# Phase stage of a four-layer kernel: sums and residual moved to GpSimd, gates and branch weights in column strips, all engine orders rewritten

## What is computed

```python
pos_cos, pos_sin = cos(pos_phases[:L]), sin(pos_phases[:L])
pos_values = x @ Wpv + bpv
pos_mem_cos = cumsum(pos_cos * pos_values, axis=1)
pos_mem_sin = cumsum(pos_sin * pos_values, axis=1)
pos_ret = (pos_cos * pos_mem_cos + pos_sin * pos_mem_sin) / sqrtD
key_ph = tanh(x @ Wk + bk) * pi
key_cos, key_sin = cos(key_ph), sin(key_ph)
kv_values = x @ Wkv + bkv
gh = gelu(concatenate([x, _shift1(x)], -1) @ Wg1 + bg1)
value_gates = sigmoid(gh @ Wg2 + bg2)                      # one number per token
kv_mem_cos = cumsum(_shift1(key_cos) * kv_values * value_gates, axis=1)
kv_mem_sin = cumsum(_shift1(key_sin) * kv_values * value_gates, axis=1)
gate_cumsum = maximum(cumsum(value_gates, axis=1), 1.0)
kv_ret = (key_cos * kv_mem_cos + key_sin * kv_mem_sin) / (sqrt(gate_cumsum) * sqrtD)
bw = softmax(gelu(x @ Wb1 + bb1) @ Wb2 + bb2)              # two numbers per token
blended = bw[..., 0:1] * pos_ret + bw[..., 1:2] * kv_ret
ln = (blended - mean) / sqrt(var + 1e-5) * ln_g + ln_b
return x + ln @ Wo + bo
```

## Time and profile before

| | |
|---|---|
| median of 3 runs | 4881.25 us (4877.01 to 4888.4) |
| profiled execution | 4887.22 us, span 4885.4 us, mean granted TensorE clock 0.962 |
| busy in the span | TensorE 4556.5, VectorE 3270.8, ScalarE 2206.4, GpSimd 1148.4 us |
| phase stage | from 2663.2 (its first DMA) to 3252.07 us (first DMA of the next stage) |

### The profile page before, as it was taken

One profiled execution on the slowest core, in us unless ns is written; L12 is line 12 of the kernel. 1 busy time (PEld: TensorE's weight loads), 2 busy tenths in 40 slices (PEclk: granted clock), 3 DMA queues, 4 the chain that ended last, 5 costly groups with the idle time before them and its releaser, 6 DMA issues. The chain is left out here.

```text
span 4885.4 us, 96760 instructions
## 1 busy us (share of the span) xinstructions
PE 4556.5 (93%) x40984; PEld 3133.7 (64%) x40984; DVE 3270.8 (67%) x3874; ACT 2206.4 (45%) x3585; POOL 1148.4 (24%) x854
## 2 busy tenths in 40 slices
PE   8699999999999996999996999949999999999999
PEld 5334444444333334888884455539999999988888
DVE  7599888887889861462223899956766666644443
ACT  3157777777677672323222555522222222233333
POOL 3512322222312202444441000003333333300000
PEclk9889999999999998999998999979999999999999
DMA  5544453544444316343344122256444444455553
GB/s 179 152 65 60 86 102 59 102 86 79 76 69 94 75 34 177 70 89 76 82 91 110 43 77 79 68 173 142 101 101 101 101 101 101 101 185 191 180 197 105
DMA packets 430317, 508.23 MB, mean 104 GB/s; under 512 B 29200, under 2 KB 361104, under 8 KB 421520
## 3 DMA queue, kind: packets, MB, share of 16 engines
q1 hardware_dynamic: 272272, 402.57, 31.3%
q10 hardware_dynamic: 133120, 67.12, 7.8%
q0 software_dynamic: 24576, 33.57, 4.2%
HBM read 250.25 MB, written 202.57 MB: 93 GB/s over the span
## 5 line engine op out<-in xcount | busy, mean ns | idle before, releaser
L974 DVE TENSOR_REDUCE att_nmx<-att_s 128x1 f32<-128x1024 f32 x1024 | 1206.4, 1216 | 183.1 <-PE att_s L797 178.8
L951 ACT ACTIVATE att_pt<-att_sT 128x512 f32<-128x512 f32 x2048 | 1083.2, 604 | 430.2 <-PE att_sT L853 426.8
L797 PE MATMUL att_s<-att_KT,att_QT 96*32 96x512 bf16 x8192 | 816.3, 393 | 92.5 <-DVE att_nmx L974 46.2
L853 PE MATMUL att_sT<-att_QT,att_KT 128*32 128x512 bf16 x8192 | 812.4, 384 | 6.2 <-ACT att_pt L951 4.9
L2658 POOL TENSOR_TENSOR sl_lg<-sl_lg,sl_sm 128x512 f32<-128x512 f32 x256 | 319.6, 1269 | 1318.8 <-DVE sl_sm L2808 1318.8
L868 PE MATMUL att_o<-att_pt,att_va 128*32 128x512 f32 x4096 | 540.5, 602 | 0.0
L797 PEld LDWEIGHTS att_s<-att_KT,att_QT 96*32 96x32 bf16 x8192 | 217.3, 97 | 494.8 <-DVE att_nmx L974 280.2
L2669 PE MATMUL sl_lp<-sl_phi,hand_big 128*128 (+1 forms) x4096 | 484.7, 277 | 30.9 <-DMA hand_big<-xnT 23.6
L2669 PEld LDWEIGHTS sl_lp<-sl_phi,hand_big 128*128 128x128 f32 x4096 | 472.2, 194 | 37.8 <-issue 35.9
L2915 PE MATMUL cb_op<-hand_big,cb_exT 128*128 128x256 f32 x2048 | 483.9, 380 | 0.0
L2733 ACT ACTIVATE sl_lg<-sl_lg 128x1024 f32<-128x1024 f32 x128 | 135.3, 1057 | 762.8 <-DVE sl_lg L2797 762.8
(11 more groups left out here) (312 smaller groups left out, 6201.0 us busy)
## 6 DMA issues: line engine op xcount, KB each, us to landing
lg<-sl_raw ACTq DMA_DIRECT2D x128, 512.0 KB, 6.0
hand_big<-lg SPq DMA_DIRECT2D x64, 1024.0 KB, 6.1
qk<-qkv_turned SPq DMA_DIRECT2D x64, 256.0 KB, 3.0
att_qin<-qk SPq DMA_DIRECT2D x64, 256.0 KB, 9.3
sl_w<-in_L_ffn_W SPq DMA_DIRECT2D x64, 256.0 KB, 3.6
y<-sl_y SPq DMA_DIRECT2D x16, 1024.0 KB, 6.9
hand_big<-y SPq DMA_DIRECT2D x7, 2048.0 KB, 8.5
att_QT<-att_hi SPq DMA_DIRECT2D x96, 128.0 KB, 4.4
```

Source lines behind the costliest of these rows:

```text
L797: ins = pe.matmul(bank[w * 32:(w + 1) * 32, q, :], QT[n % NB][0:ROWS, h, t * P + w * 32:t * P + (w + 1) * 32], KT[n % NB][0:ROWS, h, q * 5 ...
L853: ins = pe.matmul(sT[w * 32:(w + 1) * 32, at % 3, :], KT[g % NB][:, h, kt * P + w * 32:kt * P + (w + 1) * 32], QT[g % NB][:, h, step // 4 ...
L951: act.activation(pt[:, step % 2, h, c, :], sT[:, at % 3, :], ACT.Exp, scale=HD ** -0.5).then_inc(exp_done, 1)
L974: dve.tensor_reduce(nmx[n % 2][:, t, h:h + 1], s[i % 2][:].rearrange("p c k -> p (c k)"), AX.X, ALU.max, negate=True).then_inc(freed, 1)
```

## The change

- `sum_up` on VectorE no longer adds `pa`+`pb` and `ka`+`kb`: GpSimd does both, per half, in `sums`. `pa`, `pb`, `ka`, `kb` exist once per half.
- The output is scaled by ScalarE out of PSUM into a new tensor `scaled` (`scaled_outputs`), and GpSimd adds it to the residual in one operation over 128x2048 (`residual_added`). VectorE keeps the reciprocal.
- `gate` and `z` are made as four strips: quarter `j` of the tokens goes to partitions `32 j` to `32 j + 31`, with 32 weight columns. Gates, their scan, roots and weights are then 256 columns long instead of 1024. The scan's carry from strip to strip is a product with a matrix of ones above the diagonal blocks (`below`, product `carry`). To come back to one row on all partitions, gates and weights are stored to DRAM by SyncE and loaded broadcast (`gates_spread`, `shares_spread`), each store waited for first.
- The bank table and all orders are new. The pipeline is one batch deeper: in turn `p` the first half of batch `p`, the second half of `p - 1` on VectorE, and the end of batch `p - 2`; loops run to `B + 1`.

```diff
-    SPREAD = {"wo": "Z", "mean": "Z", "outA": "W", "outB": "X", "var": "Y", "k1": "Z", "gh0": "Y", "kv1": "Z", "pv1": "W",
-              "gh1": "X", "bh": "Y", "trA": "W", "trB": "Y", "gate": "Z", "z": "X", "k0": "W", "kv0": "X", "pv0": "Y"}
+    SPREAD = {"wo": "X", "var": "Y", "outB": "X", "k0": "Y", "pv0": "W", "kv0": "Y", "bh": "X", "gh1": "W", "k1": "Y",
+              "kv1": "Z", "pv1": "W", "gh0": "Y", "trA": "X", "trB": "Z", "mean": "X", "outA": "W",
+              "gate": "Z", "carry": "Z", "z": "Z"}
...
+        named = ([(n, p - 2) for n in ("var", "outB")] + [(n, p) for n in ("k0", "carry", "pv0", "kv0", "bh")]
+                 + [("gh1", p + 1)] + [(n, p) for n in ("z", "k1", "kv1", "pv1")] + [("gh0", p + 1)]
+                 + [("trA", p - 2), ("trB", p - 2), ("mean", p - 1), ("gate", p + 1), ("outA", p - 1)])
...
+                def gates_spread(p):
+                    gone(sp, ("gate", p))
+                    sp.dma_start(gate_d[p].rearrange("(w n) -> w n", n=TW), gt4[0:P:32, :]).then_inc(gate_stored, 16)
+                    sp.wait_ge(gate_stored, FLOOR + 16 * (p + 1))
+                    if p >= 1:
+                        gone(sp, ("kv1", p - 1))
+                    sp.dma_start(gt[:], col_bcast(gate_d[p])).then_inc(gate_in, 16)
+                def shares_spread(p):
+                    sp.wait_ge(w1_ready, FLOOR + p + 1)
+                    sp.dma_start(share_d[p].rearrange("(a w n) -> w a n", a=2, n=TW), w4[0:P:32]).then_inc(share_stored, 16)
+                    sp.wait_ge(share_stored, FLOOR + 16 * (p + 1))
+                    if p >= 2:
+                        sp.wait_ge(weighted, FLOOR + 4 * (p - 1))
+                    sp.dma_start(w[p % 2][:].rearrange("p a n -> p (a n)"), col_bcast(share_d[p])).then_inc(share_in, 16)
...
+                for p in range(B + 2):
+                    if p >= 2:
+                        sp.wait_ge(added, FLOOR + p - 1)
+                        sp.dma_start(rows(out_d, p - 2), base[p % 2][:]).then_inc(x3_stored, 16)
+                    if p + 2 < B:
+                        channels_in(p + 2)
+                    if p < B:
+                        shares_spread(p)
+                    if p >= 2:
+                        sp.wait_ge(xn_ready, FLOOR + p - 1)
+                        sp.dma_start(rows(xn3_d, p - 2), xn[:]).then_inc(xn_stored, 16)
+                        if p < B:
+                            residual_in(p)
...
+                    if p + 1 < B:
+                        gates_spread(p + 1)
...
+                def sums(mo, p):
+                    u = 2 * p + mo
+                    pool.wait_ge(pos_turned, FLOOR + u + 1)
+                    pool.tensor_tensor(pa[mo][:], pa[mo][:], pb[mo][:], ALU.add).then_inc(pos_summed, 1)
+                    pool.wait_ge(kv_turned, FLOOR + u + 1)
+                    pool.tensor_tensor(ka[mo][:], ka[mo][:], kb[mo][:], ALU.add).then_inc(kv_summed, 1)
+                def residual_added(p):
+                    pool.wait_ge(nat_in, FLOOR + 16 * (p + 1))
+                    gone(pool, ("outA", p))
+                    gone(pool, ("outB", p))
+                    pool.tensor_tensor(base[p % 2][:], base[p % 2][:], scaled[:], ALU.add).then_inc(added, 1)
+                for p in range(B + 1):
+                    if p < B:
+                        sums(0, p)
+                    if p >= 1:
+                        residual_added(p - 1)
+                    if p < B:
+                        sums(1, p)
...
+                    for k in range(KD):
+                        for j in range(W):
+                            ins = pe.matmul(q[32 * j:32 * (j + 1), GATE], wg2_s[:, k, 0:32], gh[:, k, j * TW:(j + 1) * TW],
+                                            start=k == 0, stop=k == KD - 1)
...
+                def scaled_outputs(p):
+                    act.wait_ge(rstd_ready, FLOOR + p + 1)
...
+                            ins = act.activation(scaled[:, tt, :], q[:, t, :], ACT.Copy, scale=rstd[:, tt:tt + 1])
```

More of the change, by code:

```diff
@@ L2028, in _ @@
                 channels_in(1)
+                sp.dma_start(ident[:], ident_d).then_inc(ident_in, 16)
                 residual_in(0)
[L2030 to L2040, removed]
+                residual_in(1)
@@ L2155, in _ @@
-                ins.then_inc(made[bank["wo", 0]], 1)
-                hidden(1, 0)
-                branch(0)
-                pe.wait_ge(columns, FLOOR + 1)
-                gate(0)
-                blend(0)
-                projected("k0", 0)
-                projected("kv0", 0)
-                gone(pe, ("wo", 0))
-                pe.wait_ge(ident_in, FLOOR + 16)
-                for p in range(B + 1):
-                    if p >= 1:
-                        mean(p - 1)
-                        outputs("outA", p - 1)
-                        outputs("outB", p - 1)
-                        variance(p - 1)
-                    if p < B:
+                pe.wait_ge(zeroed, FLOOR + 3)
@@ new lines, in _ @@
+                for p in range(-1, B + 2):
+                    now, ahead, last, old = p in range(B), p + 1 in range(B), p - 1 in range(B), p - 2 in range(B)
+                    if old:
+                        variance(p - 2)
+                        outputs("outB", p - 2)
+                    if now:
+                        if p == 0:
+                            pe.wait_ge(main_in, FLOOR + 48)
+                            pe.wait_ge(branch_in, FLOOR + 16)
+                        projected("k0", p)
+                        carry(p)
+                        projected("pv0", p)
+                        projected("kv0", p)
+                        branch(p)
+                    if ahead:
+                        if p == -1:
+                            pe.wait_ge(front_in, FLOOR + 16)
+                        pe.wait_ge(x_in[(p + 1) % 2], FLOOR + 32 * ((p + 1) // 2 + 1))
+                        hidden(1, p + 1)
+                    if now:
+                        blend(p)
@@ L2185, in _ @@
-                    if p + 1 < B:
-                        gate(p + 1)
-                        blend(p + 1)
-                        projected("k0", p + 1)
-                        projected("kv0", p + 1)
-                        projected("pv0", p + 1)
+                    if ahead:
+                        hidden(0, p + 1)
+                    if old:
+                        if p == 2:
+                            pe.wait_ge(ident_in, FLOOR + 16)
+                        turn("trA", p - 2)
+                        turn("trB", p - 2)
@@ new lines, in _ @@
+                    if last:
+                        mean(p - 1)
+                    if ahead:
+                        if p == -1:
+                            pe.wait_ge(columns, FLOOR + 1)
+                        gate(p + 1)
+                    if last:
+                        if p == 1:
+                            gone(pe, ("wo", 0))
+                        outputs("outA", p - 1)
+                    if p == -1:
+                        pe.wait_ge(wo_ready, FLOOR + 1)
+                        room(("wo", 0))
+                        for k in range(KD):
+                            ins = pe.matmul(ps[bank["wo", 0]][:, 1, 0:D], avg[:], wo_s[:, k, :], start=k == 0, stop=k == KD - 1)
+                        ins.then_inc(made[bank["wo", 0]], 1)
```

314 lines of the change are left out of this document (152 added, 162 removed).

## The result

The changed kernel takes **4900.96 us** (median of 9 runs, 4899.2 to 4906.0); the kernel before, on the same chip, 4884.41 us (9 runs, 4877.01 to 4891.22). The ratio is 1.0038, with a 95% interval of 1.0027 to 1.0048: slower by 0.4%, where 4873 and most likely faster were forecast. The time lies inside the range (4822 to 4902), near its upper end; the direction is wrong.

What follows compares the result with a forecast made beforehand. VectorE was taken to bound the stage, TensorE 4 us behind. Turns of 53.3 + 10.0 = 63.3 us, with fill and drain, gave -8.4 us; 4887.2 - 8.4 - 6.0 = 4873 us, range 4822 to 4902.

Steps and rivals of the forecast that it cites:

- VectorE's own work: In the changed stage, VectorE's work per turn of the batch loop falls from 63.8 to 53.3 us.
- GpSimd's cost: GpSimd's four sums and residual keep out VectorE operations with both inputs in SBUF, costing VectorE 10.0 us a turn.
- Case 1: GpSimd gets in at VectorE's next boundary, costing 8.5 to 12.5 us a turn; 4862 to 4892 us; chance 0.50.
- The fifth: The key sum of half 1 lies beside VectorE's `rotate(0)`, which hides it: no cost to VectorE.
- VectorE's waits: VectorE's turn was taken as 53.3 us of work plus 10.0 lost to GpSimd, 63.3 us, with no other wait.
- TensorE's floor: TensorE's least time per turn: 55.9 us of work, 57.5 with 1 to 2 us of low clock behind `var`.
- DMAs: SyncE's stores and broadcasts of gates and weights land before they are wanted: hidden, with 7 us to spare.
- Fill and drain: Stage's start and end: second half of batch 0 blended at 2771; time behind the last blend 41.7 to 44.8 us, +3.1.
- The sum: Stage end: 2771 + 6 turns x 63.3 + last turn = 3199; + 44.8 = 3243.7, against 3252.1: -8.4 us.
- the third: GpSimd's 14.1 us a turn are wholly exposed on VectorE: +31 us on the forecast, 4904; chance 0.10.
- The second rival: GpSimd gets in only beside exempt VectorE operations, or nothing is excluded: -52 us, 4829; chance 0.32.
- the fourth: Gates' broadcast lands late, as SyncE waits for a store, then a 4 MB backlog: +32 us, 4905; chance 0.08.

## Why the prediction was wrong, point by point

- **VectorE's own work**, forecast 53.3 us a turn: 53.05. Right, with its terms (the scan of 256 columns 0.55 start to start, the carry's pair 0.45, the outputs and sums gone).
- **GpSimd's cost, the step that failed first.** Case 1 held in kind: GpSimd gets in at the next boundary, even between independent products. That it came true is in part luck, since the earlier trace rows do not show it: GpSimd's indirect DMA waited for L1667 there, but L1670, right behind it (2585.43), takes its plain 1.22 us beside the rest of it and was not held up. Of its five terms four were right (forecast 2.3, 1.0, 4.5, 2.3; measured 2.16, 0.86, 4.22, 2.15). The fifth, "Key sum: `rotate(0)` hides it", was not: 2.12 us. The carry's `tensor_scalar` stands in front of `rotate(0)`, and the prediction listed it as exempt with the carry's pair, having taken only operations with both inputs in SBUF as kept out. It takes 2.47 us beside the key sum and 0.35 otherwise; the exchange of the two gave 13 us back, with part of the 2.12 us a turn lost again to waits. No row of before showed that form beside GpSimd, so it was an unmarked guess and belonged in the range with a price. The page that the prediction cites says more than it took from it: "SBUF — State Buffer", section "Who interferes with whom", of the Trainium skill has `tensor_scalar` among the operations that can enter a mode with both ports and so contend, beside those with two SBUF inputs, and exempts one-input operations outside of it. The trace agrees on both: 2.47 against 0.35, and bn_stats at 2.70 beside an addition of 2.35.
- **VectorE's waits, the step that failed second.** The walk through VectorE's turn let nothing wait. outB was moved behind the variance, which the prediction priced as 0.3 us of TensorE, 1 to 2 us of low clock in TensorE's floor and 1.5 us in the drain, but at nothing in VectorE's turn; but `sum_up(0)` must not overwrite the blend before outB has read it, and outB runs at the lower clock there (5.39 instead of 3.70). That put TensorE's chain square, variance, outB ahead of VectorE's first weighting: 5.9 us in four turns, and 14 us of the whole with what followed from it, shown by the second blend tile. The prediction named the low clock in "var, outB, k0" among what would make it wrong. In the kernel before, outB stood ahead of the variance, and it was `k1` behind it that ran at the low clock (6.00 us).
- **TensorE's floor**, forecast 57.5: 57.93, in the run with GpSimd's operations cut. It was counted with `gate` at 0.43 us and `z` at 0.21; they take 1.00 and 0.57 start to start. The earlier trace rows had it: 8 products of 512 columns in strips, 1.03 us, and `gate` is as many columns (16 records of 256), not half as many.
- **DMAs**, forecast hidden: right. The shares' broadcast landed in 6.1 us, the gates' in time.
- **Fill and drain.** The fill was 1.6 us longer than walked. The drain was 48.9 us instead of 44.8. 1.4 of the 4.1 us lie in front of the reciprocal: `mean` starts 4.1 us behind the last blend, since `trA` and `trB` of the batch before stand ahead of it on TensorE, which the prediction did not walk (it then takes 3.69 us, not the 6.35 of the earlier trace rows). 2.6 lie behind it: outB takes 6.63 us, with ScalarE's last copies behind it. The prediction's own terms of the drain add up to +2.8, not +3.1.
- **The sum.** Forecast for the profile: a stage of 580.5 us. Measured 603.8, 23.3 more: six turns 15.5, drain 4.1, last turn 1.9, fill 1.6. Another 3.2 lie outside the stage, 1.6 between profile and median. Each us of a turn being worth 7.55, GpSimd's extra 1.5 us are 11 of the 28. Of the 15.5 in the six turns 9.1 are GpSimd's, 7.9 are VectorE's waits (395.3 less 6 x 64.56), and VectorE's own work took 1.5 less than forecast.
- **The rivals.** The turning point of the third (a cost from 11.1 us a turn on makes it slower) fits the run with two blend tiles: GpSimd's 11.5 us without the waits gave a ratio of 1.0006, no more than level. Its time, 4904, is right by luck: it belongs to a cost of 14.1, and what was measured is 11.5 with waits. Its mechanism held only in part: the residual does push the position sum of half 1 in front of L2460, but the key sum missed `rotate(0)` through the carry. The second rival (GpSimd in only beside exempt operations) and the fourth (late gates) did not happen. GpSimd was busy 131 us in the stage, not 113: a position sum waits 0.9 us for VectorE's running product, inside its recorded length, and the residual takes 5.07 us.
- **Where the gain went.** Strips and new orders without GpSimd's work take 4863 against 4883: a gain of some 20 us. Sums and residual on GpSimd together then lose 38, of which the residual alone loses 14 and the sums alone nothing.

## What to carry to other kernels

In these runs, work moved from VectorE to GpSimd was only gone where it lay beside VectorE operations with an input in PSUM (or statistics). Beside the other forms seen here (two-input products and sums, scans and `tensor_scalar`, all in SBUF) VectorE paid most of the length that GpSimd took: 2.1 to 4.2 us for what it did itself in 1.1 to 3.4. So count each operation by its neighbour in VectorE's order, and place it by exchanging neighbours first. Two moves that are harmless or cheap alone can be dear together, so try each alone as well as both. When an order is rewritten, follow every tile that is overwritten as well as every one that is read: two costly surprises here (the blend behind outB, kv1's bank behind trB) were reads that came late.

## What the runs showed that was not expected

- A scan is kept out too, and keeps GpSimd out: 4.38 for 2.27, while the addition took 4.18 for 2.35.
- Who gets in is not fixed by the start. GpSimd's sum, recorded 0.16 us behind the start of L2459's product, got in at its end each time in half 0 and in the changed kernel's half 1; in the version with the outputs on VectorE the sum of half 1, at the same distance (2990.09 against 2989.93), had to wait for one product more, in seven of eight batches. Why is open; no run tests it.
- outB, behind the variance's one-column products, took 5.39 us in some turns and 3.70 in others of the same kernel; what decides it the runs do not show.
